# Carrying the gate's eight columns through the products of a graph kernel instead of normalising, turning and multiplying its last rows

## The chip, the cores and the metric

The kernel runs on one core of a Trainium2 chip. The metric is the time of one execution on the device in microseconds; the time before is the median of three runs. TensorE multiplies matrices out of SBUF into the eight banks of PSUM; VectorE, ScalarE and POOL (GpSimd) work element by element, SyncE issues transfers. The engines run side by side and meet at semaphores.

## The reference

There are 64 graphs of 256 nodes with 256 features. Each goes through two layers, and a mixture of experts ends the second:

```python
# layer 0
x = x + _L0_gnn_ref(_layernorm(x), adj, W, a)             # softmax(leaky(s1+s2), masked by adj) @ (xn @ W)
x = x + _L0_ffn_ref(_layernorm(x), W_in, ...)             # Mamba-2 block, ends in (Y * rsqrt(mean(Y*Y)+eps) * norm_w) @ W_out @ W_lin + b_lin
# layer 1
x = x + _L1_gnn_ref(_layernorm(x), ..., adj, weight, bias)  # sum over r of (adj == r+1) @ xn @ weight[r], + bias
x = x + _L1_ffn_ref(_layernorm(x), gate_w, gate_b, w1, ...) # eight experts
# inside _L1_ffn_ref, h being the normalised rows
logits = x @ gate_w + gate_b
probs = jax.nn.softmax(logits, axis=-1)
idx = jnp.argmax(probs, axis=-1)
```

`_layernorm(x)` is (x - mean) / sqrt(var + 1e-5) over the 256 features. The layers of the first three stages each add a product to x. With gate_w made free of its column means (gwc = gate_w less the mean over its 256 rows), the logits of a row x are (x @ gwc) / std + gate_b, without the row's mean.

## The kernel before

Nodes lie on the 128 partitions in T = 2 tiles, features in DK = 2 blocks of 128. The work on a graph is cut into three stages, and in one step of the loop three graphs are under way: `b1_` in stage 1 (attention), `b2_` in stage 2 (the Mamba block), `b3_` in stage 3 (relations, row statistics, gate). `rounds` (line 352) issues the steps; the loop `Fori` holds two of them, and in the second `route` (line 809) gives the last two graphs' rows their slots in the experts. Behind the loop, `tiles` runs 71 groups of 256 rows through the experts.

Each engine has its own function `step`, whose order is written out by hand; semaphores (`x1_ready`, `hp_made` and so on) join the engines. fp32 products are two TensorE instructions each in the profile, so "x8" is four calls of `mm`.

Around the change a step goes like this. TensorE makes the relation products of stage 3 (`relate`, line 1098, both tiles side by side in bank 6), the exponents of stage 2 (`expo`), the attention product of stage 1 (line 1249, both tiles in bank 1), the scan's products (line 1260), and then projects the next graph (`attend`, line 1086, tile 0 and tile 1, 258 columns: wh, s1 and s2). Between these two halves it turns `xn3`, the normalised rows of stage 3 (line 1271); behind them it turns `xn1` (line 1276), makes the gate's products from `xn3T` (line 1281) and then the output product of stage 2 (line 1289, eight calls, both tiles in bank 4), whose fifth to eighth feature block waits for the second half of `y` (`yz_ready`). VectorE in the same stretch adds stage 3's rows (line 930), takes their mean and variance (`deviation(3)`), makes `x1` (line 949), its statistics, then normalises stage 3's rows into `xn3` and stage 1's into `xn1` (`normalise`, line 786), makes `y` and multiplies it with silu(z) (lines 966, 971), adds the gate's bias (line 978), and in every second step routes. 1/std is made on POOL (`rsqrt`, line 449). ScalarE copies `xn3T` and `xn1T` out of PSUM (lines 701, 706). A row goes to DRAM with its mean, 1/std, weight and a spare number behind its 256 features (`ROW = D + 4`); the experts gather such rows.

## Time and profile before

| | us |
|---|---|
| median of three runs (3669.29 to 3671.39) | 3670.32 |
| profiled execution | 3668.25 |
| its span, first to last instruction | 3666.5 |
| busy: TensorE (share of the span) | 3470.5 (95%) |
| busy: VectorE | 2562.8 (70%) |
| busy: ScalarE | 1776.8 (48%) |
| busy: POOL | 1808.5 (49%) |
| granted TensorE clock, mean | 0.990 |

Durations come from that one execution. In the forty slices of the page (92 us each) TensorE is busy in nine tenths and more of each but the first and the one where the graphs end and the experts begin, near 2600 us. The chain of work that ended last is 51% TensorE, 26% VectorE, 12% POOL. Matmuls overlap, so the time from one group's start to the next one's tells more than the durations; "idle before" in brackets names whom an engine waited for.

### The profile page before, as it was taken

Reading aid. Unit: us, or ns where it says so; the run is one execution under the profiler, and the core shown is the slowest. Engines: PE = TensorE matmul, PEld = TensorE weight load, DVE = VectorE, ACT = ScalarE, POOL = GpSimd, SP = SyncE. Lnnn points to the kernel's source line nnn. Section 1 sums busy time; section 2 is a strip of 40 time slices with the busy share of each in tenths; the row PEclk is TensorE's granted clock in tenths of the full one; section 3 lists DMA queues with packets and bytes.
Section 4 is the critical chain, followed back from the end, with each engine's and each line's share of the span. In section 5 each row is a group of like instructions: output and inputs, shape, how many; then the busy total and the mean of one; then the engine's idle time right before and its main releaser. Section 6 shows DMA issues by size and latency. Waiting matters only on the chain.

```text
span 3666.5 us, 64685 instructions
## 1 busy us (share of the span) xinstructions
PE 3470.5 (95%) x20028; PEld 2838.1 (77%) x20028; DVE 2562.8 (70%) x7429; ACT 1776.8 (48%) x3627; POOL 1808.5 (49%) x2010
## 2 busy tenths in 40 slices
PE   7999999999999999999999999999699999999998
PEld 5777777777777777777777777777488888888887
DVE  5878888887888888788888878888444444444444
ACT  4556655655655555565565556555232323323232
POOL 3545554454554545545454554545354555545453
PEclk8999999999999999999999999999799999999999
DMA  3121111111111111111111111111155555556563
GB/s 104 39 46 36 35 40 43 37 42 41 37 38 40 40 37 46 37 37 40 37 42 35 46 37 37 40 38 33 58 199 194 196 190 193 193 192 197 194 196 128
DMA packets 166001, 301.92 MB, mean 82 GB/s; under 512 B 37376, under 2 KB 138240, under 8 KB 147776
## 3 DMA queue, kind: packets, MB, share of 16 engines
q0 software_dynamic: 38272, 196.40, 15.7%
q1 hardware_dynamic: 91536, 70.58, 6.3%
q10 hardware_dynamic: 36144, 34.35, 6.0%
q8 instruction: 24, 0.39, 0.0%
q14 instruction: 25, 0.20, 0.0%
HBM read 248.61 MB, written 52.65 MB: 82 GB/s over the span
## 4 chain that ended last, share of the span: by engine, by line
PE 51%; DVE 26%; POOL 12%; issue 8%; ACT 1%; DVEq 0%; DMA 0%; ACTq 0%; POOLq 0%; SPq 0%
PE bank L1337 13%; PE bank L1351 13%; PE bank L1083 7%; POOL masks L466 7%; DVE conv L798 6%; PE bank L1101 5%; PE bank L1189 4%; DVE y L966 3%; PE bank L1289 3%; DVE y L971 2%; POOL row L452 2%; POOL rstd L452 2%; DVE stats L779 2%; DVE xn L789 1%; PE bank L1220 1%
## 5 line engine op out<-in xcount | busy, mean ns | idle before, releaser
L732 ACT ACTIVATE decay<-bank,w_up 128x256 f32<-128x256 f32 x568 | 269.4, 474 | 700.3 <-PE bank L1337 694.5
L1083 PE MATMUL bank<-xn1T,w_in 128*128 128x256 f32 x2304 | 523.4, 381 | 15.3 <-issue 14.3
L1337 PE MATMUL bank<-zs,w_up 128*128 128x256 f32 x2272 | 504.6, 380 | 0.6 <-ACT zs L590 0.6
L1351 PE MATMUL bank<-w_dn,decay 128*128 128x256 f32 x2272 | 502.1, 379 | 0.0
L1101 PE MATMUL bank<-w_rel,hT 128*128 128x256 f32 x2048 | 492.7, 384 | 0.0
L1083 PEld LDWEIGHTS bank<-xn1T,w_in 128*128 128x128 f32 x2304 | 434.1, 190 | 72.3 <-issue 14.0
L798 DVE SCALAR_TENSOR_TENSOR conv<-bank,conv_w,conv 128x255 f32<-128x255 f32 (+2 forms) x960 | 461.3, 481 | 34.8
L1337 PEld LDWEIGHTS bank<-zs,w_up 128*128 128x128 f32 x2272 | 433.4, 191 | 60.3 <-issue 0.9
L1351 PEld LDWEIGHTS bank<-w_dn,decay 128*128 128x128 f32 x2272 | 426.2, 190 | 55.1
L1044 DVE TENSOR_TENSOR hT<-bank,w_dn 128x256 f32<-128x256 f32 x142 | 60.3, 424 | 537.1 <-PE bank L1351 537.1
L1101 PEld LDWEIGHTS bank<-w_rel,hT 128*128 128x128 f32 x2048 | 368.9, 190 | 62.8 <-ACT hT L590 13.0
L466 POOL TENSOR_SCALAR masks<-adjt_sb 128x512 fp32r<-128x512 int32 x256 | 404.3, 1596 | 5.4
L452 POOL TENSOR_TENSOR rstd<-ve,mhalf 128x2 f32<-128x2 f32 x256 | 191.7, 749 | 381.6 <-DVE ve L784 256.3
L505 POOL TENSOR_TENSOR x2b<-x,b_rel 128x256 f32<-128x256 f32 x128 | 90.1, 725 | 544.6 <-DVE xdt L920 540.3
L806 DVE TENSOR_TENSOR decay<-decay,g 128x768 f32<-128x768 f32 x256 | 247.7, 1008 | 155.0 <-ACT decay L698 155.0
L346 POOL TENSOR_TENSOR beats<-mhalf 128x1 f32<-128x1 f32 x403 | 85.3, 212 | 453.6 <-DVE hT L1044 335.7
L1189 PE MATMUL bank<-masks,xp 128*128 128x512 f32 x1024 | 273.3, 410 | 14.0 <-ACT xp L590 7.1
L1289 PE MATMUL bank<-w_proj,y 128*128 128x256 f32 x1024 | 256.6, 394 | 23.8 <-DVE y L971 23.8
L698 ACT ACTIVATE decay<-bank 128x384 f32<-128x384 f32 x512 | 209.8, 496 | 95.1 <-PE bank L1127 95.1
L1189 PEld LDWEIGHTS bank<-masks,xp 128*128 128x128 f32 x1024 | 184.0, 189 | 89.0 <-ACT hT L590 32.2
L1289 PEld LDWEIGHTS bank<-w_proj,y 128*128 128x128 f32 x1024 | 186.1, 191 | 69.7 <-DVE y L971 48.9
L520 POOL TENSOR_TENSOR y2h<-y 128x512 f32<-128x512 f32 x64 | 81.0, 1265 | 293.2 <-ACT y L711 293.2
(219 smaller groups left out, 6341.4 us busy)
## 6 DMA issues: line engine op xcount, KB each, us to landing
token_rows<-row SPq DMA_DIRECT2D x64, 258.0 KB, 2.7
xT_sb<-in_xT ACTq DMA_DIRECT2D x64, 256.0 KB
x_sb<-in_x ACTq DMA_DIRECT2D x64, 256.0 KB, 2.7
adj_sb<-in_adj SPq DMA_DIRECT2D x64, 256.0 KB, 3.0
adjt_sb<-in_adjT SPq DMA_DIRECT2D x64, 256.0 KB, 3.0
out<-row SPq DMA_DIRECT2D x64, 256.0 KB, 2.2
w_in<-token_rows,idc POOLq DMA_INDIRECT x142
out<-hT,ids POOLq DMA_INDIRECT x142
```

The costliest lines, as they stand in the source:

```text
L452: gp.tensor_tensor(rstd[i][:], ve[i][:], mhalf[:], ALU.pow).then_inc(rstd_ready[i], 1)
L466: ins = gp.tensor_scalar(masks[:, :, r, :], adjt[:], float(r + 1), None, ALU.is_equal)
L698: nc.scalar.activation(decay[:, h, :], bank[EXPO[h % 4]][:, 0:TRI], ACT.Exp).then_inc(decay_ready, 1)
L732: nc.scalar.activation(hid(f), bank[f % 4][:, 0:GROUP], ACT.Relu, bias=b1[q % 2][:, f:f + 1]).then_inc(hid_ready, 1)
L798: v.scalar_tensor_tensor(conv[:, c, k:N], src[:, 0:N - k], conv_w[:, c, TAPS - 1 - k:TAPS - k], conv[:, c, k:N], ALU.mult, ALU.add).then_i ...
L806: v.tensor_tensor(decay[:, 2 * j:2 * j + 2, :], decay[:, 2 * j:2 * j + 2, :], g[:, 0:TRI].unsqueeze(1).broadcast_to([P, 2, TRI]), ALU.mult ...
L1083: ins = mm(dst, w_in[:, k, first:first + P], xn1T[:, k, :], start=k == 0, stop=k == DK - 1)
L1101: ins = mm(bank[6][:, t * D:(t + 1) * D], hT[:, d, r * N + t * P:r * N + (t + 1) * P], w_rel[:, r, d, :], start=r == 0 and d == 0, stop=r ...
L1189: ins = mm(bank[6 + c][:, :], xp[part][:, t, d * P:(d + 1) * P], masks[:, t, 2 * c:2 * c + 2, :], start=t == 0 and part == 0, stop=t == T ...
L1289: ins = mm(bank[4][:, t * D:(t + 1) * D], y[:, j, t * P:(t + 1) * P], w_proj[:, j, :], start=j == 0, stop=j == XB - 1)
L1337: ins = mm(bank[f % 4][:, 0:GROUP], w1[i][:, k, f * P:(f + 1) * P], xgT[:, k, :], start=k == 0, stop=k == DK - 1)
L1351: ins = mm(bank[4 + j][:, 0:D], hid(f)[:, j * P:(j + 1) * P], w2[i][:, f, :], start=f == 0, stop=f == FB - 1)
```

## The change

The eight columns x @ gwc ride along with every x: x, x1, x2, x1b, x2b and the row have GX = 264 columns. Since each stage adds a product to x, the last matrix of each product gets eight more columns, its own product with gwc:

- `w_gc` (stage 1) has 274 columns: 256 of W, eight of W @ gwc, s1, s2, and gwc itself. `attend` makes all of them; ScalarE copies the eight of gwc from PSUM into x's last columns, ahead of each half of wh, and wh has 264 columns.
- `w_proj`, `w_rel`, `b_lin` and `b_rel` have 264 columns. The added ones are made once, in the first two steps, by small TensorE products from transposed weights, which three more loads bring in (W, W_lin and the relation weights, transposed on the host).
- Two tiles of 264 columns do not fit a bank: the attention product uses banks 0 and 1, the output product 4 and 2, the relation products 6 and 7. So the second tile's relation products wait for z (bank 7 held s2), and the first half of `attend` waits for x1.
- In each step `xn3`, its four turns, ScalarE's copy and the gate's products (four calls) are gone; the logits are two operations of eight columns on VectorE, ahead of normalising x1.

```diff
+    GX = D + E
+    ROW = GX + 4
...
-        WS = D + 2
+        WS = GX + 2 + E
...
         gat_loads = [
-            (w_gat, by_tile(io["L0_gnn_W"])),
+            (gate_w, by_tile(io["L1_ffn_gate_w"])),
+            (w_gat[:, :, 0:D], by_tile(io["L0_gnn_W"])),
+            (w_gatT, by_tile(io["gnn_WT"])),
             (a_bc, io["L0_gnn_a"].rearrange("(a d) o -> (a o) d", a=2).partition_broadcast(P)),
         ]
...
                     need(act, hp_made, b1_)
+                    need(act, x1_ready, b1_)
                     for t in range(T):
-                        ins = nc.scalar.activation(wh[:, t, :], bank[t][:, 0:D], ACT.Copy, scale=rstd[0][:, t:t + 1])
+                        copy(x[:, t, D:GX], bank[t][:, GX + 2:WS])
+                        ins = nc.scalar.activation(wh[:, t, :], bank[t][:, 0:GX], ACT.Copy, scale=rstd[0][:, t:t + 1])
...
-                if b3_ is not None:
-                    act.wait_ge(xn3_turned, b3_ + 1)
-                    copy(xn3T[:], bank[7][:, :]).then_inc(xn3T_ready, 1)
...
+                if is_first(b2_):
+                    dve.wait_ge(more_made, 1)
+                    v.tensor_copy(w_rel[:, :, :, D:GX], bank[6][:, REL:REL + R * DK * E].rearrange(
+                        "p (r k e) -> p r k e", r=R, k=DK))
+                    v.tensor_copy(w_proj[:, :, D:GX], bank[6][:, PROJ:PROJ + XB * E].rearrange(
+                        "p (c e) -> p c e", c=XB)).then_inc(more_ready, 1)
...
-                    ins = v.tensor_tensor(row[:, :, 0:D], bank[6][:, :].rearrange("p (t d) -> p t d", t=T), x2b[:],
-                                          ALU.add)
+                    ins = v.tensor_tensor(row[:, :, 0:GX], bank67[:, :, 0:GX], x2b[:], ALU.add)
...
-                    need(dve, xn3_turned, b3_)
-                    normalise(3, xn3, row[:, :, 0:D], xn3_ready, b3_)
+                    dve.wait_ge(rstd_ready[3], b3_ + 1)
+                    for t in range(T):
+                        ins = v.scalar_tensor_tensor(lg[:, T * turn_[1] + t, :], row[:, t, D:GX], row[:, t, GX + 1:GX + 2],
+                                                     gate_b[:, t, :], ALU.mult, ALU.add)
+                    ins.then_inc(lg_in, 1)
...
-                    dve.wait_ge(gate_made, b3_ + 1)
-                    ins = v.tensor_tensor(lg[:, T * i:T * (i + 1), :], bank[6][:, 0:T * E].rearrange("p (t e) -> p t e", t=T),
-                                          gate_b[:], ALU.add)
-                    ins.then_inc(lg_in, 1)
...
+            pe.wait_ge(gwc_ready, 1)
+            for i in range(DK):
+                for k in range(DK):
+                    ins = mm(bank[6][:, (1 + i) * E:(2 + i) * E], w_gatT[:, k, i * P:(i + 1) * P], gwc[:, k, :],
+                             start=k == 0, stop=k == DK - 1)
+            ins.then_inc(gat_more_made, 1)
...
+                    for r in range(R):
+                        for i in range(DK):
+                            for k in range(DK):
+                                j = REL + (r * DK + i) * E
+                                ins = mm(bank[6][:, j:j + E], w_relT[:, r, k, i * P:(i + 1) * P], gwc[:, k, :],
+                                         start=k == 0, stop=k == DK - 1)
...
                 if t == 0:
                     pe.wait_ge(xt_in, 16 * (b + 1))
-                    need(pe, probT_ready, b)
-                else:
                     need(pe, x1_ready, b)
...
-                        ins = mm(bank[6][:, t * D:(t + 1) * D], hT[:, d, r * N + t * P:r * N + (t + 1) * P],
+                        ins = mm(bank[6 + t][:, 0:GX], hT[:, d, r * N + t * P:r * N + (t + 1) * P],
                                  w_rel[:, r, d, :], start=r == 0 and d == 0, stop=r == R - 1 and d == DK - 1)
...
+                    if b1_ is not None:
+                        pe.wait_ge(z_ready, b1_ + 1)
                     relate(1, range(0, 2))
...
-                            ins = mm(bank[1][:, t * D:(t + 1) * D], probT[:, k, t * P:(t + 1) * P], wh[:, k, :],
+                            ins = mm(bank[t][:, 0:GX], probT[:, k, t * P:(t + 1) * P], wh[:, k, :],
...
-                if b3_ is not None:
-                    pe.wait_ge(xn3_ready, b3_ + 1)
-                    if b1_ is not None:
-                        pe.wait_ge(z_ready, b1_ + 1)
-                    turn_pair(bank[7], xn3).then_inc(xn3_turned, 1)
...
-                if b3_ is not None:
-                    pe.wait_ge(xn3T_ready, b3_ + 1)
-                    for u in range(T):
-                        for k in range(DK):
-                            ins = mm(bank[6][:, u * E:(u + 1) * E], xn3T[:, k, u * P:(u + 1) * P],
-                                     gate_w[:, k, :], start=k == 0, stop=k == DK - 1)
-                    ins.then_inc(gate_made, 1)
...
-                            ins = mm(bank[4][:, t * D:(t + 1) * D], y[:, j, t * P:(t + 1) * P], w_proj[:, j, :],
+                            ins = mm(bank[(4, 2)[t]][:, 0:GX], y[:, j, t * P:(t + 1) * P], w_proj[:, j, :],
                                      start=j == 0, stop=j == XB - 1)
```

TensorE in a step without routing, from the last products of the scan to the sum of squares; before:

```order
L1260 MATMUL bank<-decay,xdt 64x128 x2
L1094 MATMUL bank<-w_gc,xT_sb 128x258 x2
L1078 MATMUL bank<-identf,xn 128x128 x4
L1094 MATMUL bank<-w_gc,xT_sb 128x258 x2
L1078 MATMUL bank<-identf,xn 128x128 x4
L1281 MATMUL bank<-gate_w,xn3T 128x8 x4
L1289 MATMUL bank<-w_proj,y 128x256 x8
L1296 MATMUL bank<-ones_row,y2s 128x1 x2
```

and now:

```order
L1333 MATMUL bank<-decay,xdt 64x128 x2
L1142 MATMUL bank<-w_gc,xT_sb 128x274 x4
L1128 MATMUL bank<-identf,xn 128x128 x4
L1350 MATMUL bank<-w_proj,y 128x264 x8
L1357 MATMUL bank<-ones_row,y2s 128x1 x2
```

The first of the two turns and the gate's products are gone, the two halves of the projection stand together, and between them and the output product only the turn of xn1 is left.

VectorE in the same step, from the statistics of x1 (mv, ve) to the addition of the gate's bias; before:

```order
L782 BN_AGGR mv<-stats 128x2 x2
L784 TENSOR_SCALAR ve<-mv 128x2
L789 TENSOR_SCALAR xn<-row 128x256 x2
L789 TENSOR_SCALAR xn<-x,mv,rstd 128x256 x2
L966 SCALAR_TENSOR_TENSOR y<-xs,d_col,bank 128x256 x2
L971 TENSOR_TENSOR y<-y,zs 128x512
L966 SCALAR_TENSOR_TENSOR y<-xs,d_col,bank 128x256 x2
L971 TENSOR_TENSOR y<-y,zs 128x512
L978 TENSOR_TENSOR lg<-bank,gate_b 128x16
```

and now:

```order
L811 BN_AGGR mv<-stats 128x2 x2
L813 TENSOR_SCALAR ve<-mv 128x2
L997 SCALAR_TENSOR_TENSOR lg<-row,gate_b 128x8 x2
L818 TENSOR_SCALAR xn<-x,mv,rstd 128x256 x2
L1009 SCALAR_TENSOR_TENSOR y<-xs,d_col,bank 128x256 x2
L1014 TENSOR_TENSOR y<-y,zs 128x512
L1009 SCALAR_TENSOR_TENSOR y<-xs,d_col,bank 128x256 x2
L1014 TENSOR_TENSOR y<-y,zs 128x512
```

Two operations of eight columns stand where two of 256 stood, ahead of xn1, and the addition behind y is gone.

ScalarE from z to the copy of g; before:

```order
L672 ACTIVATE z<-bank,s 128x256 x2
L676 ACTIVATE wh<-bank,rstd 128x256 x2
L678 ACT_TABLE_LOAD
L590 ACTIVATE g<-bank 128x400
L687 ACTIVATE prob,esum<-e,nmax 128x256 x2
```

and now:

```order
L689 ACTIVATE z<-bank,s 128x256 x2
L607 ACTIVATE x_sb<-bank 128x8
L695 ACTIVATE wh<-bank,rstd 128x264
L607 ACTIVATE x_sb<-bank 128x8
L695 ACTIVATE wh<-bank,rstd 128x264
L697 ACT_TABLE_LOAD
L607 ACTIVATE g<-bank 128x400
L706 ACTIVATE prob,esum<-e,nmax 128x256 x2
```

The two small copies stand ahead of wh, the table load, g and prob.

## Rows read from the trace of the kernel before

**Rows 1.** Busy time by stretch: the graph loop; us, x instructions, clock, DMA

```profile
75.00:2538.00 2463.00, 2341.82 (x14608) 1857.81 (x14606) 2003.44 (x5901) 1415.16 (x2816) 1243.61 (x1290) 1.00 0.17 39
```

**Rows 2.** Timeline of TensorE; start, us, engine, line, [idle before <- releaser]

```profile
1222.00 1.14 PE L1094 MATMUL bank<-w_gc,xT_sb 128*128 128x258 f32 x4
1223.99 0.66 PE L1078 MATMUL bank<-identf,xn 128*128 128x128 f32 x4 [0.85 <-DVE xn L789]
1224.48 1.04 PE L1094 MATMUL bank<-w_gc,xT_sb 128*128 128x258 f32 x4
...
1225.79 0.96 PE L1281 MATMUL bank<-gate_w,xn3T 128*128 128x8 f32 x8
1226.60 1.12 PE L1289 MATMUL bank<-w_proj,y 128*128 128x256 f32 x4
1228.10 2.86 PE L1289 MATMUL bank<-w_proj,y 128*128 128x256 f32 x12 [0.38 <-DVE y L971]
```

**Rows 3.** Timeline of VectorE in the same step

```profile
1223.20 0.73 DVE L789 TENSOR_SCALAR xn<-row 128x256 f32<-128x256 f32 x2
1224.29 0.74 DVE L789 TENSOR_SCALAR xn<-x,mv,rstd 128x256 f32<-128x256 f32 x2 [0.36 <-POOL rstd L452]
...
1227.35 0.69 DVE L971 TENSOR_TENSOR y<-y,zs 128x512 f32<-128x512 f32 x1
1227.96 0.17 DVE L978 TENSOR_TENSOR lg<-bank,gate_b 128x16 f32<-128x16 f32 x1
```

**Rows 4.** Timeline of POOL in the same step

```profile
1223.37 0.82 POOL L452 TENSOR_TENSOR rstd<-ve,mhalf 128x2 f32<-128x2 f32 x1 [0.18 <-DVE ve L784]
...
1231.80 0.70 POOL L452 TENSOR_TENSOR rstd<-ve,mhalf 128x2 f32<-128x2 f32 x1 [0.94 <-DVE ve L986]
```

**Rows 5.** Line 789, 110 to 2530: what VectorE waited for; us, times

```profile
  POOL rstd L452: 21.6, 60
```

**Rows 6.** Timeline of TensorE: projections of 256 columns

```profile
1233.19 7.07 PE L1083 MATMUL bank<-xn1T,w_in 128*128 128x256 f32 x32
```

**Rows 7.** Timeline of ScalarE: a plain step (1241 on), one behind routing

```profile
1241.92 0.41 ACT L647 ACTIVATE s<-bank,rstd 128x2 f32<-128x2 f32 x2
...
1247.06 0.83 ACT L672 ACTIVATE z<-bank,s 128x256 f32<-128x256 f32 x2
...
1291.08 0.50 ACT L590 ACTIVATE g<-bank 128x400 f32<-128x400 f32 x1
1291.83 0.51 ACT L687 ACTIVATE prob<-e,nmax 128x256 f32<-128x256 f32 x1 [0.24 <-DVE nmax L909]
```

**Rows 8.** Timeline of TensorE in the same two steps

```profile
1250.06 1.89 PE L1101 MATMUL bank<-w_rel,hT 128*128 128x256 f32 x8
...
1292.97 0.66 PE L1229 MATMUL bank<-identf,prob 128*128 128x128 f32 x4 [0.65 <-ACT prob L687]
```

**Rows 9.** Timeline of SyncE's queue in the prologue

```profile
15.92 1.94 SPq L321 DMA_DIRECT2D gate_w<-in_L_ffn_gate_w  x1
```

**Rows 10.** Timeline of TensorE in the second step

```profile
54.26 1.12 PE L1229 MATMUL bank<-identf,prob 128*128 128x128 f32 x4 [2.54 <-ACT prob L687]
```

**Rows 11.** TensorE by stretch: us, busy (x), clock, DMA share, GB/s

```profile
50.00:51.00 1.00, 1.00 (x6) 0.50 0.00 0
```

**Rows 12.** Timeline of VectorE in the last step of the graphs

```profile
2611.55 0.73 DVE L789 TENSOR_SCALAR xn<-row 128x256 f32<-128x256 f32 x2 [0.91 <-POOL row L452]
2615.60 0.17 DVE L978 TENSOR_TENSOR lg<-bank,gate_b 128x16 f32<-128x16 f32 x1 [3.31 <-PE bank L1281]
```

**Rows 13.** Timeline of TensorE at the end of the graphs

```profile
2543.48 1.30 PE L1078 MATMUL bank<-identf,xn 128*128 128x128 f32 x8 [2.42 <-DVE xn L789]
...
2579.10 3.19 PE L1260 MATMUL bank<-decay,xdt 128*64 128x256 f32 x32 [1.72 <-ACT decay L698]
```

**Rows 14.** TensorE by stretch at the same place; columns as in rows 11

```profile
2545.00:2546.00 1.00, 1.00 (x7) 0.53 0.00 0
...
2551.00:2552.00 1.00, 1.00 (x4) 0.56 0.00 0
```

More of the change, by code:

```diff
@@ L96, in sem @@
             return ctx.enter_context(nc.semaphore(name))
-        bank = [ctx.enter_context(nc.psum_tensor(f"bank{i}", [P, 512], F32)) for i in range(8)]
+        bank = [ctx.enter_context(nc.psum_tensor(f"bank{i}", [P, 512], F32)) for i in range(6)]
+        bank67 = ctx.enter_context(nc.psum_tensor("bank67", [P, 2, 512], F32))
+        bank += [bank67[:, i, :] for i in range(2)]
         rows_d = nc.dram_tensor("token_rows", [NT, ROW], F32, kind="Internal").ap()
@@ L1139, in step @@
                     if b3_ is not None:
-                        need(pe, lg_in, b3_)
+                        need(pe, x3_ready, b3_)
                     project(bank[6][:, 0:N], DIN + DIN)
@@ L1237, in step @@
                     ins.then_inc(w_out_turned, 1)
+                    for i in range(DK):
+                        for k in range(DK):
+                            mm(bank[6][:, (3 + i) * E:(4 + i) * E], w_linT[:, k, i * P:(i + 1) * P], gwc[:, k, :],
+                               start=k == 0, stop=k == DK - 1)
+                    for i in range(2):
+                        for k in range(DK):
+                            ins = mm(bank[6][:, (5 + i) * E:(6 + i) * E], b_cols[:, i, k:k + 1].broadcast_to([P, P]),
+                                     gwc[:, k, :], start=k == 0, stop=k == DK - 1)
+                    ins.then_inc(lin_more_made, 1)
                 if b2_ is not None:
```

132 lines of the change are left out of this document (89 added, 43 removed).

## The prediction

> **What bounds the kernel now.** I read the busy time by stretch first. In the stretch that holds the graph loop TensorE is busy 2341.8 of 2463 us, 95%, at the full clock [rows 1]; the experts behind it keep it wholly busy and the change leaves their work alone. A share of 95% would make every microsecond taken from TensorE a gain. So the timelines came next, one step of the loop on each engine (a step is some 40 us; two make a round of the loop, and the second one routes). They say otherwise at just the place of the change. TensorE stands still for 0.85 us ahead of the turn of the third stage's rows, does both turns, the second half of the next projection and the gate's products, and stands still again for 0.38 us ahead of the output product's last twelve instructions, at 1228.10 [rows 2]. What ends that wait is VectorE's second product with silu(z), started at 1227.35 [rows 3]. VectorE has been without a pause since its xn1 at 1224.29, and xn1 waited for POOL's 1/std [rows 3, 4]; it did so 60 times, 21.6 us in all, 0.36 us each [rows 5]. So the chain through this place is VectorE and POOL, and TensorE's 1.3 us of gate work lie inside a wait. From 1228.10 to the exponents of the next step the chain is TensorE's own.
>
> **What goes.** On TensorE the four turns of xn3 and eight gate instructions: 0.49 us (1223.99 to 1224.48) and 0.81 us (1225.79 to 1226.60) [rows 2], 1.30 us a step and 83 us over 64 graphs. None of it is on the chain: after the change TensorE has done both halves of the projection by 1222.00 + 4 x 0.44 = 1223.8 (the same four-instruction group twice, 0.88 us each), turns xn1 when it comes at 1225.0, and then waits for the first half of y at 1226.5 and, as now, for the second at 1228.10. On VectorE normalising row goes, 0.73 us [rows 3]. But it fills the time in which POOL makes 1/std of x1; VectorE waits 0.36 us behind it. The two small logit operations (about 0.17 us each, the length of the removed addition) take its place, and xn1 starts where it did. Only POOL's own operation may become shorter: 0.82 us beside the removed normalising, 0.70 us where VectorE is idle [rows 4]. I take -0.1 us a step. The addition of the bias behind y, 0.17 us, goes from VectorE too [rows 3]. In a step without routing 3.4 us of idle time follow it there. In one with routing the chain would start 0.17 us sooner, but it soon takes the slot counts from TensorE (bank 7, line 836), whose products stand behind the output product: nothing is won.
>
> **What is added in each step.** A column costs TensorE at most 7.07 us / 32 / 256 = 0.86 ns in each instruction [rows 6], so eight cost 6.9 ns. On the chain lie twelve instructions of the output product and 24 of the relation products ahead of the exponents: 36 x 6.9 = 0.25 us. The other eight relation instructions, the attention's and the projection's lie where VectorE or ScalarE is waited for. ScalarE gets two copies of eight columns ahead of its table load: 0.41 us, by the two of two columns [rows 7]. In a step without routing prob ends some 0.25 us ahead of TensorE's need and TensorE itself comes 0.25 us later, so they are hidden. In a step behind routing prob starts 0.24 us after g is done, waits for VectorE's nmax [rows 7], and TensorE has waited 0.65 us for it [rows 8]: 0.41 - 0.24, with g also ahead of xdt, gives +0.2 us. Wider x1, x2, row and x2b: two to three times 0.017 us, +0.1 us a round with POOL's. A round: 0.25 - 0.1 (plain step), 0.08 (output product ahead of the slot counts) + 0.2 + 0.1 - 0.1 (routing), +0.42 to 0.5 us. The bound of one side is zero if ScalarE's copies hide, of the other 1.2 us if nothing does. I take 0.48 us x 31 rounds = +15 us (0 to 37).
>
> The new wait of the second relation half on z: z is done at 1247.9 where TensorE arrives at 1250.1 [rows 7, 8]; nothing. The projection's first half waits for x1, which ends at 1222.0, where TensorE starts it today [rows 2]; a delay of 0.1 us there has the hole behind it. The rows that go to DRAM grow by 3%; nobody in the loop waits for them.
>
> **What is added once.** The prologue is one chain, with TensorE and the load it waits for at its head. Ahead of the first projection: gate_w, whose issue alone took SyncE 1.94 us [rows 9], now stands before the loads that the first product waits for, with a quarter of a megabyte besides: +2.4 us. Then 16 small instructions on TensorE and four on VectorE in series, some +2.2 us. A small product costs 0.101 us at full clock (0.81 / 8) [rows 2] and 0.2 us at half, and the clock is at half in much of the prologue [rows 11]. Sixteen more stand ahead of the first attention product: +3.2 us. ScalarE's copies +0.4. In the second step 48 more stand ahead of prob's turn, 4.8 to 9.6 us, against 2.54 us that TensorE waits there now [rows 10], and xdt waits for them: +2.9 to +7.6 us. They use few columns, so I take the half clock. Together +16 us (10 to 18). By the Trainium skill (TensorE: Matmul & The Clock Gate, Back-to-back issue gap) such a small matmul could issue every 25 ns or so, which would make the prologue's 80 only 2 us; the row shows 0.101 us for them, near the weight load that the same page puts at columns / 1.2 (section LDWEIGHTS), so the trace decides.
>
> At the end of the graphs it gains: in the last step nothing hides the path from 1/std to the logits. Normalising starts at 2611.55 and the addition at 2615.60 [rows 12]; now the logits start at 2611.55. That is -3.9 us, and about -1 us in the step before. Sum without any change of the clock: +15 + 16 - 5 = +26 us.
>
> **The clock.** Taking work out of a wait widens the wait. TensorE's hole in each step grows from 0.85 us, with turns and gate products about it, to 2.8 us (1223.8 to 1226.6) that hold only four turns, and 0.38 us more soon after. The trace has one such place: in the last step with a first stage TensorE waits 2.42 us, does eight turns and the gate's products, and the granted clock falls from 1.00 to 0.50 (2.4 to 1.2 GHz) at about 2545.05, until 2551.9 [rows 13, 14]; in a loop step, wait included, the output product's sixteen instructions take 1.50 + 2.86 = 4.36 us [rows 2]. At 50 us it is at half too, behind small and narrow instructions [rows 11]. On the other side stands a wait of 1.72 us ahead of 2579 with no fall [rows 13], and none in 2463 us of the loop. The new hole lies nearer to the cases that fell. A fall costs half of the time at half clock behind 1228.1, and nothing of what falls into the wait. The stretch at 2545 lasted 6.8 us, but its first part went by on the gate's small products; here full-width products follow at once, so I take 3.4 us, which cost at most 1.7 us and, less what falls into the wait, 1.3. It needs to meet the hole at the right moment (the fall at 2545 came 1.6 us after the wait had ended at 2543.48), so not every step has it. I take a third of 62 steps: 20 x 1.3 = +27 us; the ends are 0 and 62 x 1.7 = 105 us.
> By the Trainium skill (same page, section Why this matters for your kernels) a kernel should keep idle gaps between bursts of matmuls short lest the clock go back to half; the rows at 2541 to 2552 agree, and the loop's shorter holes, without a fall, do not speak against it.
>
> **Forecast.** +26 + 27 = +53 us. The profiled execution took 3668.3 us, within 2.1 us of the median of 3670.3, so both lead to 3722 us.
>
> **Rivals.**
> 1. The clock holds. For it: 60 holes of 0.85 us and one of 1.72 us without a fall. Against: the fall behind 2.42 us. Then 3670 + 26 = 3696 us.
> 2. The clock falls in most steps, or stays low for 6.8 us as at 2545. Then 50 x 1.7 us or more: 3670 + 26 + 85 = 3781 us.
> 3. Faster: TensorE is the bound after all, since something it does earlier now (the turn of xn1, 0.4 us sooner) starts ScalarE and the next step's work sooner. It decides from the point where xn1, and y behind it, come sooner by more than the 0.25 us that the chain gets longer; the full price needs 0.8 us. Then TensorE's whole balance counts: 1.30 us less 72 instructions with eight more columns (0.50 us), 62 x -0.8 = -50, +11 for both ends: 3631 us. Against it: 60 of 60 waits of xn1 for POOL [rows 5], a POOL operation that starts only when VectorE's variance is there.
> 4. The costs per round are hidden too and the prologue is at its low end: 3670 + 10 - 5 = 3675 us.
>
> **Chances.** Forecast (a fall in some steps, 3705 to 3750) 0.5; clock holds (3680 to 3705) 0.25; falls in most (above 3750) 0.12; hidden costs 0.05; faster 0.08. About 0.2%, 7 us, is what a measurement of this kernel can tell from no change. Faster by more than that 0.08, within it 0.05, slower 0.87. The range 3680 to 3775 leaves out the hidden costs, the faster case and a part of the second rival; the forecast's own is 3705 to 3750.
>
> **What would show it.** The wait at the output product's last twelve instructions stays at about 0.38 us, or less in steps at half clock, and a new one of about 1.1 us stands at its first four; xn1 still waits for POOL, now some 0.7 us behind the small logits, and y follows at the same distance. TensorE's busy share in the loop falls by three points. The granted clock of some slices of the loop is below 1.00, in stretches of 3 us and more that begin just behind the hole. The first exponents of the second step come some 16 us later than 55.2, the last logits' chain ends 5 us nearer to the graphs' end. The forecast is wrong if the loop's rounds are shorter than 79.9 us, if the clock is 1.00 throughout, or if xn1 starts at once behind the logits.

## The result, and the profile after

| | before | after |
|---|---|---|
| median of five runs (range), us | 3671.39 (3669.29 to 3672.18) | 3689.85 (3688.42 to 3692.86) |
| ratio to before, 95% interval | | 1.0052 (1.004 to 1.0064) |
| profiled execution / its span, us | 3668.25 / 3666.5 | 3692.86 / 3691.1 |
| granted clock, mean | 0.990 | 0.985 |

The change costs 18.5 us. The forecast was 3722 us, +52: right in sign, nearly three times too large. The first rival (the clock holds, 3696 us) was nearer. The spans differ by 24.6 us; the profiled execution of after lies 3.0 us above its median and that of before 3.1 us below, which leaves 18.5.

The hole first. TensorE after, one step; columns as in [rows 2]:

```profile
1241.34 2.09 PE L1142 MATMUL bank<-w_gc,xT_sb 128*128 128x274 f32 x8
1244.22 0.66 PE L1128 MATMUL bank<-identf,xn 128*128 128x128 f32 x4 [0.79 <-DVE xn L818]
1245.73 1.16 PE L1350 MATMUL bank<-w_proj,y 128*128 128x264 f32 x4 [0.85 <-DVE y L1014]
1247.23 2.94 PE L1350 MATMUL bank<-w_proj,y 128*128 128x264 f32 x12 [0.35 <-DVE y L1014]
1250.04 0.61 PE L1357 MATMUL bank<-ones_row,y2s 128*128 128x1 f32 x4
```

It stands where it was forecast, somewhat narrower: from the end of the projection (1243.43) to the output product (1245.73) it is 2.3 us and not 2.8, the waits about the turn of xn1 are 0.79 and 0.85 us (the second was forecast at 1.1), and ahead of the last twelve instructions stand 0.35 us where [rows 2] have 0.38. VectorE in the same step, and who held it over the loop (line 818, 110 to 2550 us):

```profile
1242.38 0.36 DVE L997 SCALAR_TENSOR_TENSOR lg<-row,gate_b 128x8 f32<-128x8 f32 x2
1243.43 0.73 DVE L818 TENSOR_SCALAR xn<-x,mv,rstd 128x256 f32<-128x256 f32 x2 [0.69 <-POOL rstd L468]
...
1246.49 0.69 DVE L1014 TENSOR_TENSOR y<-y,zs 128x512 f32<-128x512 f32 x1
```

```profile
  POOL rstd L468: 42.2, 61
```

The time of the removed normalising became waiting: 42.2 us against 21.6 in [rows 5]. From x1's variance to xn1 it is 1.13 us (ve at 1242.30), before 1.18 (ve at 1223.11). POOL then shows what ends the step (y2h and y2s add up y's squares for TensorE's sum of squares); after, then before:

```profile
1247.92 1.26 POOL L537 TENSOR_TENSOR y2h<-y 128x512 f32<-128x512 f32 x1 [4.60 <-ACT y L727]
1249.26 0.73 POOL L539 TENSOR_TENSOR y2s<-y2h 128x256 f32<-128x256 f32 x1
```

```profile
1230.13 0.73 POOL L522 TENSOR_TENSOR y2s<-y2h 128x256 f32<-128x256 f32 x1
```

y2s ends at 1249.99, and TensorE's sum of squares starts at 1250.04, with the output product just done; before, y2s ends at 1230.86 and the sum starts at 1230.91. So y, ScalarE's squares and POOL's two sums run level with the output product: in both kernels the sum of squares starts 2.81 us behind the twelve instructions (1247.23 to 1250.04; before 1228.10 to 1230.91), though they are eight columns wider now.

In what follows a step is counted from the start of one such sum to the next. Before, steps of 39.10 and 40.82 us alternate, a round of 79.92; after, 39.24 and 40.88, a round of 80.12. The loop thus costs +0.2 us a round, not +0.48.

The clock, over the loop and in three of the places where it fell (last columns: granted clock, DMA share, GB/s):

```profile
75.00:2538.00 2463.00, 2297.28 (x13787) 1775.00 (x13787) 1964.81 (x5801) 1367.31 (x2843) 1232.80 (x1279) 0.99 0.18 40
163.00:165.00 2.00, 2.00 (x6) 1.44 (x5) 1.44 (x7) 0.75 (x2) 1.07 (x1) 0.50 0.04 12
644.00:646.00 2.00, 2.00 (x6) 1.38 (x5) 1.44 (x7) 0.75 (x2) 0.74 (x1) 0.50 0.00 0
1327.00:1329.00 2.00, 2.00 (x6) 1.42 (x6) 0.28 (x1) 0.63 (x1) 0.98 (x1) 0.50 0.25 27
```

TensorE's 2341.8 us of [rows 1] are 2297.3 now, a share lower by two points (forecast: three). The clock record of the trace has seven stretches at half clock between 100 and 2500 us, 3.4 us each. Six of them begin 0.1 to 1.1 us behind an output product's start; the seventh begins at 2438.8, where the loop ends and TensorE has waited 2.25 us in one piece for prob. One of the six on TensorE:

```profile
1325.83 5.52 PE L1350 MATMUL bank<-w_proj,y 128*128 128x264 f32 x16 [0.85 <-DVE y L1014]
1331.18 0.50 PE L1357 MATMUL bank<-ones_row,y2s 128*128 128x1 f32 x4
```

From the product's start to the sum of squares it is 5.35 us, without a fall 4.31 (1245.73 to 1250.04): 1.04 us, of which the next step gives back 0.14 (40.74 for 40.88).

The profiled execution is the slowest of the five and has the lowest clock (0.985; the others 0.986 to 0.989), so the seven are those of one execution, and another may have had a different number.

The two ends. TensorE in the second step, then VectorE where the graphs end, and the row of before that answers to its first:

```profile
58.81 3.42 PE L1274 MATMUL bank<-w_lin,hT 128*128 128x8 f32 x16
62.08 6.97 PE L1281 MATMUL bank<-w_gc,w_up 128*128 128x8 f32 x32
68.91 1.09 PE L1293 MATMUL bank<-identf,prob 128*128 128x128 f32 x4
...
2638.29 0.71 DVE L965 TENSOR_TENSOR row<-bank,x2b 128x528 f32<-128x528 f32 x1 [12.93 <-PE bank L1149]
2641.11 0.36 DVE L997 SCALAR_TENSOR_TENSOR lg<-row,gate_b 128x8 f32<-128x8 f32 x2 [0.83 <-POOL row L468]
```

```profile
2608.68 0.69 DVE L930 TENSOR_TENSOR row<-bank,x2b 128x512 f32<-128x512 f32 x1 [12.00 <-PE bank L1101]
```

prob is turned at 68.91 (54.26 in [rows 10]). From the last row to its logits it is 2.82 us; before, 2608.68 to 2615.60 [rows 12], 6.92.

| part of the 24.6 us | forecast | profile |
|---|---|---|
| to the first sum of squares (73.37, now 87.68) | +16 | +14.3 |
| 30 rounds, without falls | +15 (31 rounds) | +5.9 |
| falls up to 2500 us, and the rest of these rounds | +27 | +7.8 |
| last three steps | -1 | +0.8 |
| behind them | -4 | -4.2 |

### The profile page after: what moved, and what is told of

It is laid out like the page before. It is cut to its first block, busy times and chain, and to the rows that moved or that the text cites. A ratio compares the mean times of both kernels' runs of the same rounds, so it can differ in the third digit from the quotient of the medians.

```text
span 3691.1 us, 63266 instructions
## 1 busy us (share of the span) xinstructions
PE 3452.6 (94%) x19340; PEld 2780.1 (75%) x19340; DVE 2537.9 (69%) x7375; ACT 1743.9 (47%) x3691; POOL 1807.0 (49%) x2010
## 4 chain that ended last, share of the span: by engine, by line
PE 53%; DVE 25%; POOL 12%; issue 9%; ACT 1%; DVEq 0%; DMA 0%; ACTq 0%; POOLq 0%; SPq 0%
PE bank L1398 13%; PE bank L1412 13%; PE bank L1133 7%; POOL masks L482 6%; DVE conv L827 6%; PE bank L1149 5%; PE bank L1237 4%; PE bank L1350 4%; DVE y L1009 3%; POOL row L468 2%; DVE y L1014 2%; POOL rstd L468 2%; DVE stats L808 2%; DVE xn L818 1%; PE bank L1268 1%
## 5 line engine op out<-in xcount | busy, mean ns | idle before, releaser
L1149 PE MATMUL bank<-w_rel,hT 128*128 128x264 f32 x2048 | 506.7, 391 | 0.0
L522 POOL TENSOR_TENSOR x2b<-x,b_rel 128x264 f32<-128x264 f32 x128 | 92.2, 741 | 551.1 <-DVE xdt L955 546.1
L1350 PE MATMUL bank<-w_proj,y 128*128 128x264 f32 x1024 | 274.6, 415 | 74.2 <-DVE y L1014 74.2
L607 ACT ACTIVATE xn1T<-bank 128x512 f32<-128x512 f32 x64 | 38.2, 597 | 445.8 <-PE bank L1128 445.8
```

The lines of the kernel that those rows point to most:

```text
L1149: ins = mm(bank[6 + t][:, 0:GX], hT[:, d, r * N + t * P:r * N + (t + 1) * P], w_rel[:, r, d, :], start=r == 0 and d == 0, stop=r == R - 1 ...
L1350: ins = mm(bank[(4, 2)[t]][:, 0:GX], y[:, j, t * P:(t + 1) * P], w_proj[:, j, :], start=j == 0, stop=j == XB - 1)
```

## The experiments

All times are medians; ratios are to the kernel before, run on the same chip, whose median was 3669.5 to 3672.3. A "fall" is a stretch at half clock between 100 and 2500 us in the trace's record, counted in the one profiled execution of each kernel. The cuts in the diffs are marked with "..."; conditions around the lines are left out.

**1. hole_filled** (the changed kernel):

```diff
+                    for i in range(2):
+                        mm(bank[7][:, 0:D], identf[:], w_in[:, i, 0:D], start=True, stop=True)
...
                     turn_pair(bank[5], xn1).then_inc(xn1_turned, 1)
+                    mm(bank[7][:, 0:D], identf[:], w_in[:, 0, 0:D], start=True, stop=True)
```

> The changed kernel with six more TensorE instructions of 256 columns into a free bank in the new hole: four ahead of the turn of xn1, two ahead of the output product; nobody reads them. Theory (few falls, about 1 us each): the loop has no fall of the clock any more, its steps are all 39.2 or 40.9 us long, and the kernel is 5 to 9 us faster than the changed one (3681 to 3685). Rival (falls cost nothing, the steps with a fall are longer for another reason): some steps of 40.2 us remain with the clock at 1.00, and the time stays at 3690. Rival (TensorE's work counts even in the hole): six instructions of 0.22 us each in 62 steps, up to 80 us slower.

3685.38 us, ratio 1.0042 (1.0028 to 1.0056). No fall but the one at the loop's exit; all steps are 39.25 or 40.87 us. Six instructions more in each step cost nothing. Against the changed kernel it is -4.5 us, just above the expected range. The intervals overlap, but the loop's steps of 40.2 us are gone with the falls behind the hole, so they were the clock's.

**2. before_hole** (the kernel before; the hole without the rest of the change):

```diff
-                    turn_pair(bank[7], xn3).then_inc(xn3_turned, 1)
...
-                            ins = mm(bank[6][:, u * E:(u + 1) * E], xn3T[:, k, u * P:(u + 1) * P],
-                                     gate_w[:, k, :], start=k == 0, stop=k == DK - 1)
...
-                    copy(xn3T[:], bank[7][:, :]).then_inc(xn3T_ready, 1)
...
+                    ins = v.tensor_tensor(lg[:, T * i:T * (i + 1), :], xn3[:, :, 0:E], gate_b[:], ALU.add)
```

> The kernel before with the hole alone: xn3 is still normalised, but its four turns, ScalarE's copy and the gate's products are left out, and the logits are taken from the first eight columns of xn3 (so the routing is another one). No wider columns, nothing added once. Theory: TensorE's 1.3 us were wholly inside the wait; rounds stay within 0.1 us of 79.9, a few steps lose 1 us to a fall of the clock, the graphs' end gains some 2 us: 3668 to 3678. Rival (the forecast's clock term): 20 falls of 1.3 us, 3690 and more. Rival (TensorE was the bound): 3600 to 3640.

3676.05 us, ratio 1.002 (1.0011 to 1.0029). The cleanest of all: steps without a fall are 39.08 and 40.81 us, within 0.02 us of before, so TensorE's 1.3 us were wholly inside the wait. And 14 falls, one in every fourth step; the mean clock is 0.982 or 0.983 in all eleven executions, so the number hardly changes from one to the next. TensorE there, and the clock in it:

```profile
1348.83 0.66 PE L1073 MATMUL bank<-identf,xn 128*128 128x128 f32 x4 [1.19 <-DVE xn L786]
1350.33 5.34 PE L1272 MATMUL bank<-w_proj,y 128*128 128x256 f32 x16 [0.85 <-DVE y L967]
```

```profile
1350.40:1353.60 3.20, 3.20 (x8) 2.50 (x9) 2.77 (x10) 1.31 (x3) 1.07 (x1) 0.50 0.00 0
```

Such a step is 39.89 us, the next 40.65: net 0.65 us a fall, 9 us in all.

**3. fill_behind and fill_ahead** (before_hole with a part of its waits filled: two instructions behind the turn, or four ahead of it):

```diff
+                    mm(bank[7][:, 0:D], identf[:], w_in[:, 0, 0:D], start=True, stop=True)   # fill_behind: behind the turn
...
+                    for i in range(2):                                                      # fill_ahead: ahead of it
+                        mm(bank[7][:, 0:D], identf[:], w_in[:, i, 0:D], start=True, stop=True)
```

> The kernel before with the hole alone (15 falls of the clock in the loop), and now two TensorE instructions of 256 columns into a free bank between the turn of xn1 and the output product, where TensorE waits 0.85 us. Theory (the clock falls by the sum of the waits around the turn, 1.06 + 0.85 + 0.38 us): with 0.44 us of it filled, few or no falls, 0 to 5, and 4 to 10 us faster than with the hole alone: 3666 to 3672. Rival (the wait of 1.06 us ahead of the turn does it): 15 falls as now, 3676.

> The kernel before with the hole alone, with four TensorE instructions of 256 columns (0.88 us) ahead of the turn of xn1, where it waits 1.06 to 1.19 us. Theory (the sum of the waits decides): no fall in the loop, 3664 as with the fill behind the turn. Rival (the pair of waits of 0.85 and 0.38 us behind the turn decides, since only narrow turns lie ahead of it): 10 and more falls, 3672 to 3676.

3664.03 us (0.9981, 0.9972 to 0.999) and 3663.09 us (0.9981, the same interval), no fall in either; the first is 2 us below its expected range. The two holes, fill_behind first:

```profile
1225.03 0.60 PE L1270 MATMUL bank<-w_in,identf 128*128 128x256 f32 x2
1226.05 1.13 PE L1276 MATMUL bank<-w_proj,y 128*128 128x256 f32 x4 [0.42 <-DVE y L967]
1227.56 2.86 PE L1276 MATMUL bank<-w_proj,y 128*128 128x256 f32 x12 [0.38 <-DVE y L967]
```

```profile
1224.67 1.03 PE L1268 MATMUL bank<-w_in,identf 128*128 128x256 f32 x4
1225.90 0.66 PE L1073 MATMUL bank<-identf,xn 128*128 128x128 f32 x4 [0.20 <-DVE xn L786]
1227.41 1.13 PE L1277 MATMUL bank<-w_proj,y 128*128 128x256 f32 x4 [0.85 <-DVE y L967]
```

Either filling is enough, so no single wait decides; the theory of the expectation (the sum) holds and its rival falls. Unfilled, the waits are 2.3 to 2.4 us in sum (1.06 or 1.19, 0.85, 0.38); fill_ahead leaves 1.4 to 1.6, fill_behind 1.9 to 2.0. The last is as much as the changed kernel has with its six falls behind the hole, so the sum of the waits is not all: what TensorE does between them, or how the steps lie, counts too, and no run separates the two. Both are also 6 to 7 us faster than before. The loop is as before; in the profiled executions the step at the loop's exit (41.2 for 42.4 us) and the stretch behind the last sum of squares (1.2 to 1.8 us) are shorter. These kernels also route by other logits, and what each is worth was not separated.

**4. wide_hole and wide_hole2** (the changed kernel, xn1 delayed on VectorE; wide_hole2 as below, wide_hole with one constant in place of the two pointers):

```diff
+                    for i in range(4):
+                        v.tensor_scalar(spare[i // 2][:, i % 2, :], x1[:, i % 2, 0:D], mv[1][:, i % 2, 0:1], mv[1][:, i % 2, 0:1],
+                                        ALU.subtract, ALU.mult)
                     normalise(1, xn1, x1, xn1_ready, b1_)
```

> The changed kernel with four operations of 256 columns (0.73 us a pair) on VectorE ahead of xn1, into tiles that nobody reads: xn1 starts 0.7 to 0.8 us later, TensorE waits 1.5 us instead of 0.79 ahead of its turn. Both theories: 62 x 0.75 = +46 us by the chain alone, 3736. Theory (the wider the hole, the more steps have a fall, each some 1 us): 20 and more falls in the loop, 3750 to 3775, mean clock 0.975 or lower. Rival (how often it falls hangs on how the steps lie, not on the width): 5 to 12 falls as before, 3736 to 3745.

> The changed kernel with four operations of 256 columns with two pointers (0.36 us each, 1.5 us in all; in the run wide_hole four cheaper ones took only 0.9 us and moved xn1 by 0.02 to 0.19 us) ahead of xn1: TensorE's wait ahead of the turn 1.5 us instead of 0.79. By the chain alone 62 x 0.6 to 0.75 us, 3690 + 37 to 46 = 3727 to 3736. Theory (the wider the hole, the more steps have a fall): 20 and more falls, 3745 to 3770, mean clock 0.978 or lower. Rival (how often it falls hangs on how the steps lie): 5 to 15 falls, 3730 to 3745.

wide_hole: 3704.2 us (1.009, 1.0075 to 1.0106), 14 falls, but its premise failed in most steps: the four operations took 0.89 us in all and widened the first wait by 0.02 or 0.19 us in 49 of 58 steps, and by 0.7 us, to 1.52, in nine. Of these nine, six have a fall, of the other 49 seven. wide_hole2: 3742.49 us (1.0193, 1.0178 to 1.0209), mean clock 0.976, 30 falls, one in each second step: as many as the theory wanted, at a time 2.5 us below its range and inside the rival's. TensorE in one of them:

```profile
1229.95 0.66 PE L1132 MATMUL bank<-identf,xn 128*128 128x128 f32 x4 [1.30 <-DVE xn L819]
1231.46 5.40 PE L1354 MATMUL bank<-w_proj,y 128*128 128x264 f32 x16 [0.85 <-DVE y L1018]
```

So the forecast's rule was right, wider falls oftener, and its rate was wrong for this width. Falls behind the hole, in some 60 steps (one more at the loop's exit in after, wide_hole, wide_hole2, narrow and no_copies):

| waits in the hole, in sum | falls |
|---|---|
| 2.0 us: no_small, after, no_copies, narrow | 2, 6, 10, 10 |
| 2.0 to 2.2 us, in nine steps 2.7: wide_hole | 13 |
| 2.3 to 2.4 us: before_hole | 14 |
| 2.5 us: wide_hole2 | 29 |

At 2.0 us the number goes from 2 to 10 with the same waits (no_small, no_copies and narrow stand below), so how the steps lie, or chance, has a part too; how large a part is open.

**5. narrow** (the changed kernel, three products at 256 columns):

```diff
-                                 w_rel[:, r, d, :], start=r == 0 and d == 0, stop=r == R - 1 and d == DK - 1)
+                                 w_rel[:, r, d, 0:D], start=r == 0 and d == 0, stop=r == R - 1 and d == DK - 1)
...
```

> The changed kernel with the attention, output and relation products at 256 columns instead of 264; the eight columns hold what lies in the banks, so the logits mean nothing. Theory (a column costs 0.86 ns in each of the 36 instructions on the chain, 0.25 us a step): 62 x 0.2 to 0.25 = 12 to 16 us faster, 3674 to 3678, rounds of 79.7. Rival (the columns are hidden too, and the +0.2 us of a round come from VectorE's and ScalarE's small additions): 3688 to 3691, rounds of 80.1.

3683.87 us, 1.0039 (1.0025 to 1.0053), 11 falls. The time misses the expected 3674 to 3678, with four falls more than after. The round is 79.53 us, 0.2 below the expected 79.7, and not for the reason given: the steps behind routing stay at 40.87 us and the others lose 0.58. In these the attention product starts 25.08 us behind the sum of squares (before: 25.08, after: 25.29), so the columns are worth 0.21 us there. The other 0.37 us come with a pair of VectorE operations (line 835), 0.43 us shorter; after first, then narrow:

```profile
1273.48 2.26 DVE L835 TENSOR_TENSOR decay<-decay,g 128x768 f32<-128x768 f32 x2 [2.45 <-ACT decay L717]
...
1272.84 4.41 POOL L482 TENSOR_SCALAR masks<-adjt_sb 128x512 fp32r<-128x512 int32 x3
```

```profile
1346.03 1.83 DVE L835 TENSOR_TENSOR decay<-decay,g 128x768 f32<-128x768 f32 x2 [2.29 <-ACT decay L717]
...
1345.55 5.11 POOL L482 TENSOR_SCALAR masks<-adjt_sb 128x512 fp32r<-128x512 int32 x3
```

VectorE's pair is 0.4 us shorter and POOL's masks beside it are 0.7 us longer, in every one of these steps. The pair starts 0.2 us sooner behind the sum of squares in narrow; that this decided who waited is argued, not tested.

**6. no_copies and no_small** (the changed kernel without ScalarE's two copies; without 44 of the 48 instructions of 8 columns in the second step, which its expectation counts as 46):

```diff
-                        copy(x[:, t, D:GX], bank[t][:, GX + 2:WS])
...
-                    for c in range(XB):
-                        for k in range(DK):
-                            mm(bank[6][:, PROJ + c * E:PROJ + (c + 1) * E], w_outT[:, k, c * P:(c + 1) * P],
-                               w_lin[:, k, D:GX], start=k == 0, stop=k == DK - 1)
...
-                    for r in range(R):
-                        for i in range(DK):
+                    for r in range(1):
+                        for i in range(1):
```

> The changed kernel without ScalarE's two copies of eight columns a step (x's last columns are zero, so the logits lack the first term). Theory (they overlap with wh, which starts 0.05 us behind each, and cost the step behind routing 0.1 us): 3 us faster, 3685 to 3688, rounds of 80.0. Rival (the forecast's price of 0.41 us less 0.24 in the step behind routing): 6 us and more, 3680 to 3684, rounds of 79.9.

> The changed kernel without the small products of w_proj and all but one of w_rel (46 of 48 instructions left out; their columns hold one block's values, so the logits are others). Theory (they stand on the prologue's chain, 10.1 us from 58.81 to 68.91 in the changed kernel, of which 2.5 us would be a wait anyway, and VectorE's copies cost a bit more here): 6 to 8 us faster, 3682 to 3684, the second step's first exponents some 7 us sooner. Rival (a wait takes their place): under 2 us.

no_copies: 3693.19 us, 1.006 (1.0046 to 1.0074), slower than both expected: it has 11 falls, and its first sum of squares comes 3.1 us later. Of these, 1.4 us stand ahead of TensorE's first product, which waits for a load (10.61 us, after 9.22), and most of the rest at a projection that took 3.91 us where after has 2.09; why is open. The clearing of x's columns, which the edit adds on POOL, takes 0.11 us. The rounds say what was asked: 80.03 us, 0.09 less than 80.12. The copies cost 0.1 us a round.

no_small: 3685.9 us, 1.004 (1.0025 to 1.0056), 4 us below after where 6 to 8 were expected, with two falls. TensorE in its second step:

```profile
60.56 0.86 PE L1277 MATMUL bank<-w_gc,w_up 128*128 128x8 f32 x4
63.21 1.11 PE L1289 MATMUL bank<-identf,prob 128*128 128x128 f32 x4 [1.79 <-ACT prob L706]
```

The stretch that took 10.1 us in after (58.81 to 68.91) takes 2.65, so the products cost 7.4 us there, and 1.8 us of it is the wait for prob that comes back. The first sum of squares is at 82.34 and not 87.68, 5.3 us sooner only, because this execution was 1.75 us behind already at 60.56: its first load came 0.4 us later and some of its first products took longer.

**7. y_first and before_y_first.** In both kernels y's first sum, which waits for nothing that xn1 brings, goes ahead of xn1:

```diff
+                if b2_ is not None:
+                    y_sum(0)
...
                 if b1_ is not None:
                     need(dve, xn1_turned, b1_)
                     normalise(1, xn1, x1, xn1_ready, b1_)
```

> The changed kernel with y's first half (scan plus D times xs, 0.86 us) ahead of xn1 on VectorE, where VectorE waits 0.69 us for 1/std. Theory (the chain from x1 over 1/std, xn1 and y to the output product sets the step): y ends 0.6 to 0.7 us sooner in each of 62 steps, 3690 - 40 = 3650, faster than both kernels. Rival (the later turn of xn1, by 0.17 us, or a later wait takes it back, as y2s on POOL): less than 10 us. Rival (the hole moves and the clock falls oftener): over 3670 with a mean clock under 0.98.

> The kernel before with y's first sum (0.86 us) ahead of xn1 on VectorE; xn3, its turns and the gate's products stay. Theory (with the gate's work in the hole, TensorE cannot use an earlier y): VectorE fills only its wait of 0.36 us, xn1 and its turn come 0.5 us later, the gate's products (0.81 us) stand behind that turn, and the output product runs without its wait of 0.38 us: a gain of 0.1 to 0.4 us a step, 3645 to 3664. Rival (the order on VectorE is all, and the change has no part in it): the same 60 us as in the changed kernel, 3610.

y_first: 3627.61 us, 0.9888 (0.9873 to 0.9903). before_y_first: 3635.03 us, 0.9904 (0.9888 to 0.9919). Both gained more than expected (3650; 3645 to 3664). VectorE of y_first:

```profile
1213.86 0.86 DVE L1005 SCALAR_TENSOR_TENSOR y<-xs,d_col,bank 128x256 f32<-128x256 f32 x2
1214.64 0.73 DVE L818 TENSOR_SCALAR xn<-x,mv,rstd 128x256 f32<-128x256 f32 x2
...
1216.79 0.69 DVE L1019 TENSOR_TENSOR y<-y,zs 128x512 f32<-128x512 f32 x1
```

xn1 starts 1.13 us behind ve as in after, with the sum inside its wait, so y ends 0.9 us sooner: steps of 38.35 and 39.98 us, -0.89 and -0.90. That settles that y sets a step. The sum of squares again starts 0.05 us behind y2s (1220.30, 1220.35), so it is y's way over ScalarE and POOL that is seen last, with the output product level with it. In before_y_first the steps are 38.52 and 40.25, since y is 0.57 us sooner there and TensorE's output product runs straight through behind the gate's products. Now the change is worth a gain, 0.44 us a round, and pays for its prologue: the two kernels are 7.4 us apart. y_first has no fall.

**8. y_ahead, before_y_ahead, y_ahead2, before_y_ahead2, y_ahead3.** All of y ahead of xn1, and the turn of xn1 inside the output product:

```diff
+                if b2_ is not None:
+                    out_part(0, range(0, 2))
+                    out_part(0, range(2, 4))
+                    out_part(1, range(0, 2))
                 if b1_ is not None:
                     pe.wait_ge(xn1_ready, b1_ + 1)
                     turn_pair(bank[5], xn1).then_inc(xn1_turned, 1)
+                if b2_ is not None:
+                    out_part(1, range(2, 4))
```

> The changed kernel with y wholly ahead of xn1 on VectorE (y's first sum even ahead of the statistics of x1), the turn of xn1 on TensorE moved in between the output product's first twelve and last four instructions, and ScalarE's squares of y ahead of its copy of xn1T. Theory (VectorE's chain through y holds TensorE, which waits 0.80 and 0.35 us a step in the version with only the first sum moved): both waits go, up to 1.1 us a step, 0.8 of it won, 3628 - 50 = 3578. Rival (xn1T now comes too late for the next projection, or y2s for the sum of squares): 3610 to 3630. Rival (the order does nothing more): 3628.

> The kernel before in the same order: y ahead of xn1, xn3 normalised between y's halves, its turns behind the first four instructions of the output product and the gate's products behind the first twelve. Theory (with the waits gone TensorE's work counts, and here it is 0.8 us a step more than in the changed kernel, VectorE's 0.5 us more): 30 to 50 us slower than the changed kernel in this order, less 11 for prologue and end: 3600 to 3620. Rival (the gate's work stays hidden in some wait): within 10 us of it or faster.

3636.88 us (0.9907, 0.9892 to 0.9922) and 3693.15 us (1.0061, 1.0048 to 1.0075): both missed, in the steps with routing by a wait that I had made. TensorE, then VectorE of y_ahead in a step with routing:

```profile
1261.18 0.18 PE L1380 MATMUL bank<-ohb,triub 128*128 128x8 bf16 x1 [0.80 <-DVE ohb L855]
```

```profile
1259.80 0.18 DVE L846 TENSOR_REDUCE gsum<-ge 128x4 f32<-128x32 f32 x1 [1.26 <-ACT ge L732]
```

ScalarE's exponentials of the routing stood behind its copy of xn1T, which now comes late. The wait brought falls too, 5 in y_ahead and 13 in before_y_ahead, all but one behind the routing's products and none behind the output product; of the three kernels below, two have one fall and one none. The next three put them ahead of it (y_ahead3 also moves y's first product ahead of x1's statistics):

```diff
+                    nc.scalar.activation(ge[:, 0:n * T, :], lg2[:, 0:n * T, :], ACT.Exp).then_inc(ge_ready, 1)
                     copy(xn1T[:], bank[5][:, :]).then_inc(xn1T_ready, 1)
-                    nc.scalar.activation(ge[:, 0:n * T, :], lg2[:, 0:n * T, :], ACT.Exp).then_inc(ge_ready, 1)
```

> y_ahead with ScalarE's exponentials of the routing ahead of its copy of xn1T. Theory (the 0.80 us that TensorE waits for the one-hot rows in each second step go, VectorE's wait of 1.26 us for the exponentials shrinks to 0.5): 0.7 to 0.9 us a round, 3637 - 22 to 28 = 3609 to 3615, rounds of 77.6. Rival (VectorE's routing is one chain and ends as late): 3630 and more.

> The same edit in the kernel before with y ahead. There the logits come only behind the gate's products, VectorE waits 2.23 us for them and 0.61 us for the exponentials. Theory: 0.3 to 0.4 us a round, 3693 - 11 = 3682, so that in this order the change is worth 65 to 75 us. Rival (it gains as much as the changed kernel, 25 us): 3668.

> y_ahead2 with the product of y's first half with silu(z) ahead of the statistics of x1 as well. Theory: TensorE's wait of 0.62 us ahead of the output product goes, that of 0.35 us ahead of its fifth instruction stays or grows by what the first one lost (VectorE has no pause between y's halves): in the steps without routing 0 to 0.3 us, 0 to 10 us in all, 3600 to 3612. Rival (xn1, 0.6 us later in relation to y, becomes late for its turn): 5 us slower than y_ahead2.

| | median, us | ratio (95%) | steps, us |
|---|---|---|---|
| y_ahead2 | 3600.96 | 0.9813 (0.98 to 0.9826) | 37.95, 39.57 |
| before_y_ahead2 | 3677.71 | 1.0024 (1.0014 to 1.0033) | 39.18, 40.98 |
| y_ahead3 | 3608.8 | 0.9838 (0.9824 to 0.9851) | 38.07, 39.69 |

y_ahead2 is the fastest of all, 69 us (1.9%) under the kernel before, and 8 us below its expected range; before_y_ahead2 is 4 us below its own, y_ahead3 inside it. In this order the change is worth 77 us, 2.64 us a round. But the order does not suit the kernel before: before_y_ahead2 is 43 us slower than before_y_first. Between the fastest of each kind, 3635.0 and 3601.0 us, the change is worth 34 us. TensorE of y_ahead2, then of before_y_ahead2:

```profile
1206.01 1.16 PE L1355 MATMUL bank<-w_proj,y 128*128 128x264 f32 x4 [0.62 <-DVE y L897]
1207.52 2.05 PE L1355 MATMUL bank<-w_proj,y 128*128 128x264 f32 x8 [0.35 <-DVE y L897]
1209.41 0.60 PE L1137 MATMUL bank<-identf,xn 128*128 128x128 f32 x4
```

```profile
1189.60 1.99 PE L1284 MATMUL bank<-w_proj,y 128*128 128x256 f32 x8 [0.59 <-DVE y L869]
1191.42 0.95 PE L1301 MATMUL bank<-gate_w,xn3T 128*128 128x8 f32 x8
1192.23 0.63 PE L1089 MATMUL bank<-identf,xn 128*128 128x128 f32 x4
```

The gate's 0.81 us (1191.42 to 1192.23) has no wait to lie in here, and VectorE's normalising of xn3 stands between y's halves and makes the second one late (0.59 us of wait for 0.35). The runs do not separate the two. This comes near the forecast's third rival, that TensorE's work counts, but only once y is out of the way. In y_ahead3, xn1 and so its turn come later in relation to y; it lost 0.25 us a round.

## Why the prediction was right and wrong

**Right.** That TensorE's 1.3 us lie inside a wait (before_hole, steps unchanged to 0.02 us); that VectorE's normalising hid behind POOL's 1/std (42.2 us of waits for 21.6); the prologue (+14.3 for 16) and the graphs' end (-3.4 in sum for -5); the place and length (3.4 us) of the stretches at half clock. The length was luck in part: I had halved the 6.8 us of the one stretch measured, with no row for a half.

**The step that failed** is the one on the clock: "I take a third of 62 steps: 20 x 1.3 = +27 us". There were 7: six behind the hole, at some 0.9 us net each (0.65 in before_hole), and one at the loop's exit, 1.6 us: 7 to 8 us in all. The rate failed, 6 of 62 steps for a third, and so did the price, 0.9 for 1.3 us. The one fall that the trace of before had at such a place [rows 13, 14] came behind 2.42 us in one piece, with 2 us of small and narrow instructions behind it; the new hole has 2.0 us in three pieces with turns and full-width products between. The experiments show how the rate grows: waits of 2.3 us in sum fell in every fourth step, of 2.5 in every second. I scaled from one event that met an unusual stretch, and took its long form as the case. By the Trainium skill (TensorE: Matmul & The Clock Gate, section Why this matters for your kernels) gaps between bursts of matmuls are to be kept short; the runs agree, and add that several short ones count together.

**A mis-sized term** is the steady loop, +15 us for +5.9. Of its parts, the columns came out right up to the attention product (+0.21 us in a step without routing; 32 x 6.9 ns), but the output product's share is hidden (2.81 us at either width), since POOL's y2s ends with it; ScalarE's copies cost 0.1 us a round and not 0.2, since the operation behind each starts 0.05 to 0.06 us after it, and the row that I priced them by [rows 7] was their duration; and the steps with routing grow by 0.06 us only. What the chain through POOL gives back is 0.05 us, not 0.1.

**What I had not looked at.** I named y as the end of the chain, but followed it to TensorE alone. The sum of squares, behind ScalarE and POOL, is as late as the output product, so y must come sooner before either can. Moving one VectorE sum of 0.86 us did that and won 62 us, three times what the whole change cost; the same move won 36 us in the kernel before.

## What to carry to other kernels

Work removed from an engine inside its wait is worth nothing until the wait is; ask first what the waiting engine's partner could do earlier, then remove: here the same edit costs 18 us in one order, gains 7 in a second and 77 in a third, and 34 between the fastest version of each kind. Compare the best order of both sides before giving an edit its price. Where an edit leaves a wait on some engine (0.69 us on VectorE), look for ready work behind it before judging the edit. A rate from one event is no rate: before a clock term carries half of a forecast, price the case in which it hardly occurs.

## What the runs showed of the hardware that I had not expected

- Filling a wait with useless full-width products is free and keeps the clock: six instructions a step took the falls from 7 to the one at the loop's exit and the time did not rise (3685.4 for 3689.9 us); in before_hole, two or four took all 14 (3664.0 and 3663.1 for 3676.1 us).
- In before_hole the falls came at equal distances, one in each fourth step, 14 times in a row; in wide_hole2 one in each second. Where the steps are this even the falls come in a fixed pattern; in after and narrow they do not.
- Beside each other, VectorE's pair of 768 columns took 2.26 us with POOL's three masks at 4.41, or 1.83 with 5.11. By the Trainium skill (SBUF — State Buffer, section Terms) the two engines share a pair of ports that one holds for a whole instruction while the other blocks; the rows agree in so far as one is longer where the other is shorter, though not by the same amount (0.7 and 0.4 us).
- Four VectorE operations of 256 columns with one constant took 0.89 us (wide_hole), the same four with two pointers 1.38 us (wide_hole2).
